# A selective-state mixer and FFN on one core: TensorE's scaled state behind the projection, its state product behind the turned tokens, VectorE's scaling just ahead of y

## The reference, cut to what matters

```python
proj = einsum('bsd,ed->bse', x, in_proj_w)            # x: 2 x 512 x 512
gate, hBC, dt = split(proj)                            # 8192, 8192 + 2*8*128, 128 channels
hBC = silu(causal_conv4(hBC) + conv_b)
hs, Bm, Cm = split(hBC)                                # 128 heads x 64; 8 groups x 128 states, twice
dt = clip(softplus(dt + dt_bias), 0, 100); A = -exp(A_log)
# in chunks of 128 tokens:
Y_diag = (C B^T * L) (hs * dt)                         # L = exp(segsum(dt*A)), lower triangle
states = B^T (decay * hs * dt)                         # one per chunk, carried with exp(A_last)
Y_off  = C prev_state * exp(A_cum)
Y = Y_diag + Y_off + hs * D
g = Y * silu(gate)
out = (g * rsqrt(mean(g*g over the group) + eps) * norm_w) @ out_proj_w.T
x = layernorm(x + out)
x = layernorm(x + x @ W.T + bias + lora(x))            # 8 LoRA adapters of rank 16
```

## Time and profile before

| | |
|---|---|
| median of 3 runs | 1669.71 us (1666.08 to 1671.05) |
| the profiled execution, whole | 1670.15 us |
| its span, first to last instruction | 1668.4 us, 26982 instructions |
| PE busy | 1615.9 us, 97% |
| PEld busy | 1292.9 us, 77% |
| DVE busy | 1346.1 us, 81% |
| ACT busy | 1221.7 us, 73% |
| POOL busy | 1025.9 us, 61% |
| DMA | 178.67 MB, mean 107 GB/s |
| mean granted clock of PE | 0.995 |

### The profile page before, as it was taken

The page is one execution under the profiler, slowest core; times in us unless marked ns, Lnnn a source line. Parts: engine busy times, 40 slices in busy tenths (PEclk is TensorE's granted clock), DMA queues, the critical chain, the costliest instruction groups (busy, mean ns, idle before and its releaser), DMA issues. The chain is left out here.

```text
span 1668.4 us, 26982 instructions
## 1 busy us (share of the span) xinstructions
PE 1615.9 (97%) x9072; PEld 1292.9 (77%) x9072; DVE 1346.1 (81%) x1855; ACT 1221.7 (73%) x2373; POOL 1025.9 (61%) x829
## 2 busy tenths in 40 slices
PE   7999999999999999999999999999999999999898
PEld 6777887778878788778877788777887778877665
DVE  5577798869987799777978689886998779887776
ACT  5768778777767876877777777788677777778742
POOL 4456667566675656656666656666576665666654
PEclk9999999999999999999999999999999999999999
DMA  3654434444454434444444443544335442445511
GB/s 124 219 119 96 115 91 120 113 107 93 95 141 97 112 95 104 113 98 118 93 109 111 107 101 93 148 88 108 96 91 143 95 124 79 108 118 95 131 32 45
DMA packets 236889, 178.67 MB, mean 107 GB/s; under 512 B 16464, under 2 KB 198736, under 8 KB 236368
## 3 DMA queue, kind: packets, MB, share of 16 engines
q1 hardware_dynamic: 235312, 175.72, 43.8%
q10 hardware_dynamic: 1440, 1.22, 0.2%
HBM read 172.17 MB, written 4.72 MB: 106 GB/s over the span
## 5 line engine op out<-in xcount | busy, mean ns | idle before, releaser
L950 POOL TENSOR_TENSOR w_lo<-raw,w_hi 128x512 fp32r<-128x512 f32 x209 | 292.6, 1400 | 312.9 <-ACT w_hi L709 311.9
L495 PE MATMUL proj<-x_hi,w_hi 128*128 128x512 f32 x1160 | 463.1, 399 | 8.7 <-DVE x_lo L1214 7.2
L496 PE MATMUL proj<-x_lo,w_hi 128*128 128x512 f32 x1160 | 453.1, 391 | 0.0
L497 PE MATMUL proj<-x_hi,w_lo 128*128 128x512 f32 x1160 | 452.8, 390 | 0.0
L1101 DVE SCALAR_TENSOR_TENSOR hs<-proj,uch,hs 128x511 f32<-128x511 f32 (+2 forms) x384 | 285.3, 744 | 54.7 <-ACT hs L736 49.4
L791 ACT ACTIVATE decay<-decay,tok 128x128 f32<-128x128 f32 x1024 | 312.4, 391 | 4.2 <-DMA decay<-acum_d 4.2
L1123 DVE TENSOR_TENSOR decay<-decay,cb 128x1024 f32<-128x1024 f32 x128 | 186.6, 1458 | 103.2 <-ACT decay L797 100.7
L1002 POOL TENSOR_TENSOR dh<-dh,eac 128x512 f32<-128x512 f32 x96 | 130.6, 1361 | 222.6 <-DVE eac L1149 222.5
L495 PEld LDWEIGHTS proj<-x_hi,w_hi 128*128 128x128 f32 x1160 | 219.0, 189 | 51.9 <-issue 6.8
L497 PEld LDWEIGHTS proj<-x_hi,w_lo 128*128 128x128 f32 x1160 | 218.4, 188 | 46.0
L496 PEld LDWEIGHTS proj<-x_lo,w_hi 128*128 128x128 f32 x1160 | 219.0, 189 | 41.5
(11 more groups left out here) (121 smaller groups left out, 2757.5 us busy)
## 6 DMA issues: line engine op xcount, KB each, us to landing
decay<-acum_d SPq DMA_DIRECT2D x128, 512.0 KB, 8.8
raw<-w_t SPq DMA_DIRECT2D x209, 256.0 KB, 6.4
eac<-eacum_d SPq DMA_DIRECT2D x192, 128.0 KB, 8.6
wo_raw<-wo_t SPq DMA_DIRECT2D x32, 256.0 KB, 7.4
c_new<-wo_t SPq DMA_DIRECT2D x32, 256.0 KB, 8.5
hs<-x_t SPq DMA_DIRECT2D x8, 256.0 KB, 5.7
acc<-x_tok SPq DMA_DIRECT2D x1, 2048.0 KB, 7.8
out<-acc SPq DMA_DIRECT2D x8, 256.0 KB, 2.0
```

Source lines behind the costliest of these rows:

```text
L495: nc.tensor.matmul(dst[:], w_hi[:, ws, k, :], x_hi[:, k, cols], start=(k == 0), stop=False)
L496: nc.tensor.matmul(dst[:], w_hi[:, ws, k, :], x_lo[:, k, cols], start=False, stop=False)
L497: mm = nc.tensor.matmul(dst[:], w_lo[:, ws, k, :], x_hi[:, k, cols], start=False, stop=(k == KC - 1))
L950: nc.gpsimd.tensor_tensor(w_lo[:, s].rearrange("p a b -> p (a b)"), raw[:, s, :], w_hi[:, s].rearrange("p a b -> p (a b)").bitcast(F32), A ...
```

## The change

PE: the scaled state moves from the head of a step to behind the first projection and norm_sum, just ahead of p_yd. The state product moves behind the next step's front. DVE: scale_off moves from the end of the step before to the step itself, behind the first taps and take_var; then comes front of the next step, and then y (at c = 0 and 4, which have nothing to scale, front stands behind y). take_var stands ahead of y in all steps. front waits for xd_ready, since xdt is overwritten. SP: load_eac is issued one step ahead in place of two, and the one in the prologue goes.

```diff
@@ SP, prologue
-            load_eac(sp, 0, 0, 1)
@@ SP, body
-                        o2, e2, c2 = ahead(e, c, 2)
-                        if c2 % CPB and not (last and o2):
-                            load_eac(sp, g + o2, e2, c2)
+                        o1, e1, c1 = ahead(e, c, 1)
+                        if c1 % CPB and not (last and o1):
+                            load_eac(sp, g + o1, e1, c1)
@@ PE, body
+                        ffn_step = last and e == 1
+                        if todo:
+                            project(g, todo.pop(0))
+
+                        if e == 1 and c > 1:
+                            norm_sum(g, c - 2, last)
+                        elif e == 0 and c < 2 and not (g == 0):
+                            norm_sum(g - 1, 6 + c, False)
+
                         if c % CPB:
 
                             pe.wait_ge(state_ready, updates(g, e, c - 1))
...
                             mm.then_inc(yoff_ready, 1)
-                        ffn_step = last and e == 1
-                        if todo:
-                            project(g, todo.pop(0))
-
-                        if e == 1 and c > 1:
-                            norm_sum(g, c - 2, last)
-                        elif e == 0 and c < 2 and not (g == 0):
-                            norm_sum(g - 1, 6 + c, False)
...
                         mm.then_inc(yd_ready, 1)
+                        off, ne, ncn = after(e, c)
+                        if not (last and off):
+                            front(g + off, ne, ncn)
                         if c % CPB != CPB - 1:
                             pe.wait_ge(xd_ready, updates(g, e, c))
                             wait(pe, yoff_scaled, carried(g, e, c))
                             nc.tensor.matmul(p_st[:], b_tok[:, c, :], xd[:].rearrange("p a b -> p (a b)"),
                                              start=True, stop=True).then_inc(st_ready, 1)
-                        off, ne, ncn = after(e, c)
-                        if not (last and off):
-                            front(g + off, ne, ncn)
@@ DVE, front
                 dve.wait_ge(hid_ready, step(g, e, c) + 1)
+                wait(dve, xd_ready, carried(g, e, c))
@@ DVE, body
-                        if e == 1 and c == 7:
-                            take_var(g, 5)
+                        if e == 1 and c > 1:
+                            take_var(g, c - 2)
                         elif e == 0 and c < 2 and g > 0:
                             take_var(g - 1, 6 + c)
+                        if c % CPB:
+                            scale_off(g, e, c)
+                            if more:
+                                front(g + off, ne, ncn)
...
                         nc.vector.tensor_tensor(y[:], p_yd[:], dh[:], ALU.add).then_inc(y_ready, 1)
-                        if e == 1 and 1 < c < 7:
-                            take_var(g, c - 2)
+                        if c % CPB == 0:
+                            front(g + off, ne, ncn)
...
-                        if more:
-                            front(g + off, ne, ncn)
...
-                        if c < 7 and (c + 1) % CPB and len(STEP_TILES[e][c]) == 1:
-                            scale_off(g, e, c + 1)
...
-                        if c < 7 and (c + 1) % CPB and len(STEP_TILES[e][c]) > 1:
-                            scale_off(g, e, c + 1)
```

## The result

The changed kernel takes 1724.8 us (median of 4 runs, 1719.89 to 1729.35), the kernel before on the same chip 1667.89. The ratio is 1.0336, 95% interval 1.0317 to 1.0355. All ratios here are of fast executions; one of the four of k7 further down was slow (1805.66 us at a mean granted clock of 0.849), and its ratio leaves it out. The forecast was 1708, its range 1684 to 1728. The profiled execution took 1721.85 us with a span of 1720.1, so 51.7 more than the span of before. These 51.7 are what has to be found.

What follows compares the result with a forecast made beforehand. TensorE, busy 1615.9 of 1668.4 us, was taken as the bound, so its waits add time. 17.5 + 6.2 + 6.4 + 11.9 + 2.0 - 6.1 = +37.9 on 1670.15 gave 1708 us, range 1684 to 1728.

Steps and rivals of the forecast that it cites:

- (1,5): Half 1, chunk 5: VectorE without gaps scales late, so the state product waits 2.5 us in 7 groups, 17.5 us.
- The clock rival: The 2.5 us stall at (1,5) also lowers TensorE's clock in 7 groups, +12, giving 1720 us; chance 0.12.
- (0,1): Half 0, chunk 1: VectorE's longer chain from variance to second wo_lo pair delays the out projection 1.7 us in 7 groups, 11.9.
- GpSimd's chain from there through the weight load arrives 0.2 later: Into (0,1): GpSimd's chain, starting from ScalarE's silu of C in (1,7), arrives 0.2 us later.
- SP: the eac issue keeps its place and loses its wait for dh: In SP's queue: the eac issue stays in place and no longer waits for dh; costed at nothing.
- (1,1): Half 1, chunk 1: scaling behind the first wo_lo pair, 0.7 us in 7 groups, 1.3 in the last, 6.2 together.
- (0,5): Half 0, chunk 5: eac, issued one step ahead, lands late, so the state product waits 0.8 us in 8 groups, 6.4.
- The place of L660: On TensorE: moving the state product behind the transposes only permutes them; costed at nothing.
- Seams: On TensorE: fewer slow hand-overs between matmul kinds, a third of the 18 us bound, 6.1 us saved.
- The last half group: Steps mostly without projections, where eac lands late but VectorE lags anyway: 2 us added, bounds -2 and +6.
- The bounds of the prediction: Over all terms: all lower bounds together give +8 us (1678), all upper ones +65 (1735).

Runs made afterwards that it cites:

- k7: Changed kernel with eac loads two steps ahead, in (1,7) behind the weight loads, and (1,5)'s scaling ahead of the taps: 1693.74 us, ratio 1.0148.
- e2: Changed kernel, but in (1,5) alone VectorE scales ahead of the three taps instead of behind them: 1713.81 us, ratio 1.0258.
- k10: e1, but in (1,3) alone the scaled state heads TensorE's step and its scaling ends VectorE's step before, as before the change: 1707.07 us, ratio 1.0212.
- e1: Changed kernel with the eac loads issued two steps ahead again, as in the kernel before: 1721.56 us, ratio 1.03.
- k13: k7, but with the eac loads issued behind the weight loads in every step: 1683.37 us, ratio 1.0075.
- k9: Kernel before, with the eac load issued behind the weight loads in every step: 1653.55 us, ratio 0.991.
- e5: Changed kernel with the state product ahead of the next step's front again, right behind p_yd: 1753.89 us, ratio 1.0499.
- e4: Kernel before with the changed kernel's VectorE order alone, TensorE's order and loads as before: 1729.97 us, ratio 1.0353.

## Why the prediction was right, and where it was not

The direction, the mechanism and the main place held; the size was 38 against 52 in the profiled execution and 57 between the medians.

- **(1,5), 17.5: right.** The idle is 2.53 to 2.58 in seven groups, 17.8. e2 shows that the taps ahead of the scaling make it, k10 that the hand-over scaling, dh, y in (1,3) makes part of it.
- **The clock rival (1720, 12 in 100) came true in five groups of seven,** at 1.6 us each in the interval behind the wait, where 1.7 had been worked out from the earlier trace rows: 8 us, of which about 4 come back at (1,6). What failed is that I took 2.5 us of idle for too short to do what 2.8 had done, with no row between them but 1.5. The Trainium skill, "TensorE: Matmul & The Clock Gate", section "HAM oscillation — how this bites in real kernels", says that a wait of PE inside a loop can put it back to the low clock each time round. The 0.77 behind the wait agrees with it, and so do e1, with a fall in all seven groups, and e2, which has neither wait nor fall there; groups 0 and 1 of the kernel after, with the wait and no fall, show that it does not do so every time.
- **(0,1), +11.9: +9.5 and -9.1 measured in the two intervals, +0.4 together.** The step that failed is "GpSimd's chain from there through the weight load arrives 0.2 later", and "SP: the eac issue keeps its place and loses its wait for dh". The issue for (0,1) does not keep its place: it leaves (1,7), where it stood ahead of the weights. These land earlier, ScalarE's wait of 3.28 goes, and VectorE's chain starts earlier by about what the scaling and dh add to it. I had counted VectorE's operations in (0,1) and taken its start for given. For the order alone the term was of the right size: e1 has the loads of before and the order of after and stands 9.6 above before over the two intervals (2.4 of it in the first group), and k13, which differs from k9 in the order only, stands 13.3 above it. k9 gets 14.2 from earlier weights without the change.
- **(1,1), 6.2: 9.3 measured, and the cause named was the second one.** I put it down to the wo_lo pair at 3.29 us. The pair took 2.42 after, and VectorE then stood 1.52 for the transfer. SP issues eac for (1,1) at Y+3.8 of (1,0), before at Y+2.1 for a step later, because a weight load ahead of it in the queue waits until Y+1.5 for GpSimd's w_lo, which is now later. The prediction looked at SP's queue for (0,5) only. With the transfer out of the way (e1, k7) the pair is what the scaling stands behind, and PE waits 0.2 to 1.2 a group, around the 0.7 that had been forecast.
- **(0,5), 6.4: right in cause, 9.2 in size.** Six groups of eight wait, up to 2.2. I had taken the landing of one group, 8.6, for all of them: after, the pair of (0,4) lands after 9.1 at the latest in group 4, 10.0 in group 5 and 6.8 and 6.4 in groups 2 and 6. e1 takes 9.9 away.
- **Two waits not priced, (1,4) with +6.4 and (1,6) with +4.5.** The out projection of (1,4) waits for the half sum, which VectorE makes late in the stretch that I had seen to be without a gap; the wait of (1,6) is that of groups 0 and 1 and of the last. Together 11 us lie where the forecast had no term.
- **The place of L660.** "Putting L660 behind the transposes L507 only permutes them; I cost it at nothing" took the product for work of PE alone and not for cover. C·B in (0,0) waits for the variance once the product does not stand ahead of it, and e5 removes that wait. It was right to cost it at nothing in the sum all the same, since what the wait adds in (0,0) is missing in (0,1).
- **Seams, -6.1: mis-sized.** L495, now L494, stayed at 398 ns in the mean against 399, where I had looked for 390. In steps that nothing else touches a step is 0.05 to 0.08 shorter, in others 0.02 longer, some 0.3 a group, about 2.4 in all. The Trainium skill, the same page, section "Step-by-step: what each phase is for", says that weight loads are pulled ahead of running matmuls, and by that it would be nothing. The measured value lies nearer to that than to my third of the bound; the rows were right at each seam, but the new seam takes most of the gain back.
- **The last half group, +2.0:** it came to +2.0 from (1,1) on, with single steps between -2.8 and +2.6, so this agreement is of a sum and not of its terms. I had no row for it and ran nothing there.
- **The hs wait of (0,7), -4.1 with its seams,** was a gain that I missed, though the earlier trace rows show it: nine waits, 2.8 of 5.8 us in one of them.

The bounds of the prediction, added up as they are listed, give about +5 and +64, not +8 and +65; the stated range does not hang on them.

Errors of both signs cancelled in part: -11.5 at (0,0) and (0,1) together, +11 at waits not priced, +8 of clock, +3 each at (0,5) and (1,1). That the time lies in the stated range is therefore in part luck: had (0,1) cost its 11.9, the median would be near 1736, above the upper end of 1728.

What stays open: 0.3 a group at (1,6) beyond wait and clock; why groups 0 and 1 kept the clock behind a wait of the same 2.5 us and lost it in e1 (one execution of each kernel was profiled; the four of the kernel after have mean granted clocks of 0.987 to 0.992, so the falls may not be the same in each); and why the eac loads of (0,5) land after some 6.2 us in groups 2 and 6, which do not wait, and after 8.4 to 9.9 in groups 1 and 3 to 5 (before it was the same two groups, with 5.8 and 5.7). No kernel was made for these.

## What to carry to other kernels

An instruction that is moved for the sake of one engine takes its cover with it: list for each wait what work stood between producer and consumer, before and after, on PE as on the others. When loads move in a queue, look first at the ones behind them: here the same edit of one SP line cost 11 us where its own data were waited for and gave 9 where it stood ahead of weights. And the best version came from that side finding: leave the compute order alone and issue what is needed last behind what is needed first (1653.55 us, 0.9% faster).

## What the runs showed of the hardware that was not expected

- The same 256 KB weight load of (1,7), groups 1 to 6, lands 9.2 to 10.6 us after issue before and 7.9 to 9.7 in e1, both with two eac loads right ahead of it in the same queue, and 6.5 to 9.1 after and 7.0 to 9.5 in k9 without them. The ranges overlap; in group 3 it is 10.6 and 8.7 against 6.5 and 7.0.
- The length of a wait did not decide by itself whether the clock fell. Behind (1,5) it fell in five groups of seven after waits of 2.5 us in the kernel after, in seven of seven after the same wait in e1, in four of seven after 1.9 in e4, in none after 1.6 to 2.1 in k10 and in none after 0.24 to 0.28 in e2. In e2 it fell behind a wait of 1.76 in (0,5) and did not behind one of 2.22.
- The same wo_lo pair took 3.29 us before, with GpSimd at work from its start to its end, and 2.42 after, with GpSimd at work for 1.50 of it.
